# Layer 0 without key projection, one score fill for two key blocks, weights loaded in pieces, and another issue order

## What is computed

```python
# layer 0, per sequence: channels c = 64 tokens, positions s = 256 features, 8 heads
xn = layernorm_over_(c, s)(x) * gamma[:, None] + beta[:, None]
q  = Wq @ xn + bq                       # (8*64, 256)
k, v = split(Wkv @ ctx + bkv)           # (8*64, 256) each
att = softmax(q.T @ k / sqrt(64))       # per head, 256 x 256
x  = x + Wo @ (att @ v) + bo
# layer 1: queries from x, keys and values from layernorm(ctx), 16 heads of 16, gated
# layer 2: queries from ctx's partner x, keys and values from both (two key blocks), then an MLP
# layer 3: self-attention, cross-attention with ctx, MLP
```

## Time and profile before

| | |
|---|---|
| time, median of 3 runs | 1281.34 us (1281.11 to 1281.63) |
| span of the profiled execution, first to last instruction | 1279.4 us |
| TensorE (PE) busy | 1250.0 us, 98% |
| VectorE (DVE) busy | 1002.7 us, 78% |
| ScalarE (ACT) busy | 866.9 us, 68% |
| GpSimd (POOL) busy | 610.1 us, 48% |
| mean granted TensorE clock | 0.997 |

### The profile page before, as it was taken

The page is one execution under the profiler, slowest core; times in us unless marked ns, Lnnn a source line. Parts: engine busy times, 40 slices in busy tenths (PEclk is TensorE's granted clock), DMA queues, the critical chain, the costliest instruction groups (busy, mean ns, idle before and its releaser), DMA issues.

```text
span 1279.4 us, 35838 instructions
## 1 busy us (share of the span) xinstructions
PE 1250.0 (98%) x13338; PEld 988.7 (77%) x13338; DVE 1002.7 (78%) x2426; ACT 866.9 (68%) x2287; POOL 610.1 (48%) x1003
## 2 busy tenths in 40 slices
PE   8999999999999999999999999999999999998898
PEld 6777768777787787877878687877878787877777
DVE  4788797887888787897868878887887989676753
ACT  3777766676777677666786777677586677765452
POOL 2554454454545545554553744545454454443231
PEclk9999999999999999999999999999999999999999
DMA  9000000000000000000000000000000000000000
GB/s 340 23 19 19 1 20 7 23 8 6 19 11 20 7 22 7 7 19 11 19 6 12 20 6 20 7 11 21 10 15 11 19 7 6 3 6 2 5 6 5
DMA packets 23592, 25.82 MB, mean 20 GB/s; under 512 B 10624, under 2 KB 22912, under 8 KB 23168
## 3 DMA queue, kind: packets, MB, share of 16 engines
q1 hardware_dynamic: 22208, 22.89, 5.6%
q10 hardware_dynamic: 1216, 0.66, 0.3%
HBM read 21.44 MB, written 2.10 MB: 18 GB/s over the span
## 4 chain that ended last, share of the span: by engine, by line
PE 82%; DVE 6%; issue 4%; ACT 3%; POOL 3%; DMA 0%; POOLq 0%; ACTq 0%; DVEq 0%
PE bank L691 9%; PE bank L960 9%; PE bank L517 8%; PE attended L646 8%; PE bank L631 8%; PE bank L969 8%; PE bank L697 5%; PE bank L725 5%; PE bank L506 4%; PE bank L751 4%; PE bank L714 3%; PE bank L738 3%; PE bank L684 2%; PE bank L425 2%; PE bank L742 2%
## 5 line engine op out<-in xcount | busy, mean ns | idle before, releaser
L618 POOL TENSOR_SCALAR p_a<-p_a,rec_a 128x256 f32<-128x256 f32 x512 | 243.4, 493 | 184.3 <-DVE rec_a L573 182.8
L604 ACT ACTIVATE p_a<-bank,nmax_a 128x256 f32<-128x256 f32 x512 | 237.8, 480 | 63.3 <-DVE nmax_a L567 62.5
L567 DVE TENSOR_REDUCE nmax_a<-bank 128x2 f32<-128x512 f32 x256 | 167.0, 677 | 13.3 <-PE bank L517 12.9
L631 PE MATMUL bank<-ident,p_a 128*128 128x128 f32 x1024 | 146.1, 277 | 3.9 <-POOL p_a L618 3.5
L517 PE MATMUL bank<-k_a,q_a 64*128 64x256 f32 x1024 | 139.2, 397 | 1.5 <-ACT q_a L584 0.6
L631 PEld LDWEIGHTS bank<-ident,p_a 128*128 128x128 f32 x1024 | 115.4, 142 | 31.5 <-issue 20.9
L646 PE MATMUL attended<-p_a,v_a 128*64 128x256 f32 x1024 | 131.7, 389 | 1.8 <-DVE p_a L664 1.4
L517 PEld LDWEIGHTS bank<-k_a,q_a 64*128 64x128 f32 x1024 | 91.9, 186 | 31.0 <-issue 22.2
L679 ACT ACTIVATE p_a<-bank 128x512 f32<-128x512 f32 x128 | 77.2, 605 | 46.2 <-PE bank L631 45.2
L604 ACT ACTIVATION_READ_ACCUMULATOR p_a<-bank,nmax_a 128x1 f32 x512 | 107.9, 211 | 0.0
L646 PEld LDWEIGHTS attended<-p_a,v_a 128*64 128x64 f32 x1024 | 64.8, 136 | 49.6 <-issue 19.7
(11 more groups left out here) (263 smaller groups left out, 3034.0 us busy)
## 6 DMA issues: line engine op xcount, KB each, us to landing
wb<-in_wb SPq DMA_DIRECT2D x1, 4096.0 KB, 13.6
wc<-in_wc SPq DMA_DIRECT2D x1, 4096.0 KB, 24.0
xc<-in_x SPq DMA_DIRECT2D x16, 128.0 KB, 2.7
xc<-in_ctx SPq DMA_DIRECT2D x16, 128.0 KB, 2.9
c_top<-in_ctx SPq DMA_DIRECT2D x16, 128.0 KB, 2.8
k_c<-in_ctx SPq DMA_DIRECT2D x16, 128.0 KB, 2.0
res_a<-in_x SPq DMA_DIRECT2D x16, 128.0 KB, 2.1
out<-y_out SPq DMA_DIRECT2D x16, 128.0 KB, 1.7
```

The costliest lines, as they stand in the source:

```text
L567: dve.tensor_reduce(nmax_a[:, n, e, :], ps[:, :].rearrange("p (q k) -> p q k", q=KT), AX.X, ALU.max, negate=True).then_inc(A.s["max"], 1)
L604: last = act.activation(p_a[:, j % 2, n, e, qt, :], ps[:, qt * D:(qt + 1) * D], ACT.Exp, bias=nmax_a[:, n, e, qt:qt + 1], accum_out=sum_a[ ...
L618: last = pool.tensor_scalar(p_a[:, j % 2, n, e, qt, :], p_a[:, j % 2, n, e, qt, :], rec_a[:, n, e, qt:qt + 1], 1.0, ALU.mult, ALU.mult)
L631: last = nc.tensor.transpose(ps[:, kt * D + qt * P:kt * D + (qt + 1) * P], p_a[:, j % 2, n, e, qt, kt * P:(kt + 1) * P], ident[:, :])
```

## The change

1. **Layer 0's keys.** The setup makes `wm`, the product of each head's query and key weights (transposes of the loaded weights, line 1268, eight 64-wide matmuls, 1276), and `bq`, the key weights times the query bias (1279). x is loaded twice, into both 64-row halves of `xx`; ctx into both halves of `cc`. A new stage `q` makes the queries of a pair in two steps of two matmuls (510), ScalarE scales them (522), and line 539 scores them against the raw ctx in `cc`. The key projection and VectorE's `k_a` are gone. The queries of all four rounds have a place of their own in `q_a`; `xx` has one place instead of two.
2. **Stage `e`.** The scores of both key blocks go into the same four banks as one fill of 32 matmuls, after both blocks of keys are ready, and VectorE masks 512 columns with one instruction (the mask is spread over four heads, with zeros for the second block).
3. **Weights.** `wb` comes in eight pieces, `wc` in six; three pieces are issued by ScalarE, the others by SyncE, and each user waits for its own piece.
4. **Order.** All five order strings and the bank table are new. Filler matmuls: 13 + 62 instead of 14 + 97.

```diff
-WARM_UP = 14
-IDLE_WORK = 97
+WARM_UP = 13
+IDLE_WORK = 62
...
-    fills = [(("qk", j, 0), ("qk", j, 1)) for j in range(2)]
-    for u, j, n in units():
-        fills.append((("s", u, 0), ("s", u, 1)))
-        if n and j + 2 < H0 // 2:
-            fills.append((("qk", j + 2, 0), ("qk", j + 2, 1)))
-    return tuple(fills)
+    return tuple((("s", u, 0), ("s", u, 1)) for u, j, n in units())
...
+    "q": ((("q", 0), ("q", 1)), (("q", 2), ("q", 3))),
...
     "pe": (
-        "wwwwwwwwsnswwwwwwnnnaaaaaaddaaddddkdaasdksddnkddkdkksnaakkdddkaadddkdaddaadddnnabdadbdnadbdkddddnabadbdbdadkbd"
+        "wwwwwwwwwwwwwsnksssknnkqqanakkskdaanddkdddaadddsdnsddaddddaqddqaadkdddkkddnanaddbkbdndbdddaaddbdbddbaabkeddnee"
...
+        def pe_q(i):
+            pe, z = nc.tensor, i % 2
+            for p in range(2):
+                yield
+                if i == 0:
+                    written(X, pe, 0, ("m", 0))
+                    written(X, pe, 0, ("m", 1))
+                pe.wait_ge(N.s["norm"], N.at(i, "norm", 2))
+                for half, rows_ in enumerate((slice(0, S), slice(S, P))):
+                    ps = fill_bank(A, pe, i, ("q", 2 * p + half))
+                    filled(A, mm(ps[:, :], wm[rows_, p, :, :], xx[rows_, :, :], start=True, stop=True), i, ("q", 2 * p + half))
...
-                for half, rows_ in enumerate((slice(0, S), slice(S, P))):
-                    ps = fill_bank(A, pe, i, ("qk", j, half))
-                    filled(A, mm(ps[:, :], wqk[rows_, 2 * j:2 * j + 2, :], xc[rows_, z, :, :], start=True, stop=True), i, ("qk", j, half))
...
-                        ins = mm(bs[e][:, qt * D:(qt + 1) * D], q_a[rows_, j % 2, n, qt * P:(qt + 1) * P], k_a[rows_, j % 2, n, :],
+                        ins = mm(bs[e][:, qt * D:(qt + 1) * D], q_a[rows_, j, n, qt * P:(qt + 1) * P], cc[rows_, z, n, :],
...
-                ins = dve.tensor_scalar(k_a[:, j % 2, :, :], ps[:, :].rearrange("p (n s) -> p n s", n=2), bqk[:, 1, j:j + 1], None, ALU.add)
...
+            yield
+            written(T, pe, i, "q")
+            pe.wait_ge(T.s["kblk"], T.at(i, "kblk", 1))
+            if T is E:
+                pe.wait_ge(T.s["kblk_own"], T.at(i, "kblk_own", 1))
+            bs = [fill_bank(T, pe, i, ("s", g)) for g in range(QUADS)]
             for c in range(blocks):
-                yield
-                written(T, pe, i, "q")
-                kblk = "kblk_own" if T is E and c else "kblk"
-                pe.wait_ge(T.s[kblk], T.at(i, kblk, 1))
-                bs = [fill_bank(T, pe, i, ("s", c, g)) for g in range(QUADS)]
...
-            def masked(c, ps, dst):
-                if c == 0:
-                    return dve.scalar_tensor_tensor(dst, ps, 1.0 / HD, bc(m2[:, :], 1, HB // 2), ALU.mult, ALU.add)
-                return dve.tensor_scalar(dst, ps, 1.0 / HD, None, ALU.mult)
+            def masked(ps, dst):
+                return dve.scalar_tensor_tensor(dst, ps, 1.0 / HD, m2[:, :, :, :], ALU.mult, ALU.add)
...
-            sp.dma_start(wb[:, :], dram["wb"]).then_inc(setup["wb_in"], 16)
+            load_weights(sp, wb, "q0", "b_q0")
+            load_weights(sp, wb, "o0", "b_o0")
```

More of the change, by code:

```diff
@@ L44, with piece @@
 WCOLS = sum(a * b for a, b in WB.values())
+PIECES = {"q0": ("q0", "q0"), "kv0": ("k0", "v0"), "o0": ("o0", "o0"), "q1": ("q1", "q1"), "kv1": ("k1", "v1"), "o1": ("o1", "o1"),
+          "w1": ("w1", "w1"), "w2": ("w2", "w2"), "qkvo0": ("q0", "o0")}
+def piece(name):
+    sizes = {n: a * b for n, (a, b) in WB.items()}
+    names = list(sizes)
+    first, last = (names.index(n) for n in PIECES[name])
+    start = sum(sizes[n] for n in names[:first])
+    return slice(start, start + sum(sizes[n] for n in names[first:last + 1]))
 UNITS = H0
@@ L49 @@
 AHEAD = 4
-WARM_UP = 14
-IDLE_WORK = 97
+WARM_UP = 13
+IDLE_WORK = 62
 SHIFTED_APART = 13
 def attention_fills(blocks):
-    return (tuple(tuple(("s", c, g) for g in range(QUADS)) for c in range(blocks))
+    return ((tuple(("s", g) for g in range(QUADS)),)
             + tuple((("t", r, c),) for r in range(KT) for c in range(blocks)) + (("o",), ("p",)))
@@ L379, in place @@
         def place(T, i, name):
-            return places["d" if T is A and name[0] == "x" else T.name, i, name]
+            return places[{"x": "d", "q": "q"}.get(name[0], "a") if T is A else T.name, i, name]
         def fill_bank(T, eng, i, name):
@@ L1284, in pe_s @@
             pe = nc.tensor
+            halves = (slice(0, S), slice(S, P))
+            yield
+            pe.wait_ge(setup["consts"], IDENT)
+            pe.wait_ge(setup["wqk_in"], 32)
+            ps = fill_bank(X, pe, 0, "wT")
+            for j in range(H0 // 2):
+                last = pe.transpose(ps[:, j * P:(j + 1) * P], wqk[:, 2 * j:2 * j + 2, :].rearrange("p h o -> p (h o)"), ident[:, :])
+            filled(X, last, 0, "wT")
+            yield
+            pe.wait_ge(setup["cols_in"], 32)
+            written(X, pe, 0, "wT")
+            bs = [fill_bank(X, pe, 0, ("m", e)) for e in range(2)]
+            for j in range(H0 // 2):
+                for e, half in enumerate(halves):
+                    mm(bs[e][halves[j % 2], j // 2 * S:(j // 2 + 1) * S], wT[half, j, 0:S], wT[half, j, S:P], start=True, stop=True)
+            for j in range(H0 // 2):
+                for e, half in enumerate(halves):
+                    last = mm(bs[e][half, P + j:P + j + 1], wT[half, j, S:P], col("l0_bq")[half, 2 * j + e:2 * j + e + 1], start=True, stop=True)
+                    if j == H0 // 2 - 1:
+                        filled(X, last, 0, ("m", e))
             yield
@@ L1305, in pe_s, with load_weights @@
                 filled(X, last, 0, ("row", n + 1))
+        def load_weights(eng, tile, name, sem):
+            eng.dma_start(tile[:, piece(name)], dram["wb" if tile is wb else "wc"][:, piece(name)]).then_inc(setup[sem], 16)
         def act_s():
             yield
-            for dst, src in ((wv_raw[:, :, :], dram["wv0"]), (wo_raw[:, :, :], dram["wo0"])):
-                nc.scalar.dma_start(dst, src).then_inc(setup["wvo_in"], 16)
             for dst, src in ((wqk[0:S, :, :], dram["wq0"][0:S, :].rearrange("p (h c) -> p h c", c=P)[:, :, 0:S]),
```

403 lines of the change are left out of this document (201 added, 202 removed).

## The result

The change brings the time from 1281.49 us (median of 4 runs of the kernel before on the same chip, 1281.11 to 1282.12) to **1220.88 us** (4 runs, 1219.85 to 1221.77). The ratio is 0.9529, with a 95% interval of 0.9515 to 0.9542: 60 us faster, where 62 were forecast.

A forecast was written before the change was run, and what follows sets the result against it. TensorE, busy 1250.0 of 1279.4 us, was taken as the bound, so work removed from its middle is time. Terms -27.5 - 32 + 4 - 8.5 + 2 = -62 take 1281.3 to 1219 us, range 1207 to 1240.

The forecast's parts named there:

- the middle: From first projection to last layer-0 sum: -27.5 for the projection, -32 for switches, +2 for waits, -57.5 us in all.
- the tail: From the last layer-0 sum to the end: -8.5 us, from fewer fillers, idle time unchanged.
- The key projection: Layer 0 on TensorE: 64 of 128 wide matmuls go, 32 pairs at 0.86 us each, -27.5 us.
- Switches: TensorE's changes of tile shape fall from 660 to 454, at 0.155 us each: -32 us, the largest term.
- Rival A: Fewer tile-shape switches give little: only the drain counts, or savings return as PSUM bank waits; 1241 to 1249 us, chance 0.10.
- Setup: Start of the kernel: added weight products and transposes delay the first projection to about 21 us; net +4 us.
- Fillers: 36 fewer filler matmuls, all but one in the tail, 72 records of 0.118 us: -8.5 us.
- I let the idle time of the tail stand: End of the kernel: useful work behind the last layer-0 sum stays about the same, TensorE's idle time there too.
- Rival B: Gaps of the tail stay, 8.5 us return as idle, with clock dips: 1228, up to 1231 us; chance 0.11.
- The other engines: VectorE's dropped key copies, its wider masks, ScalarE's work and double x loads: worth nothing while TensorE bounds.
- New waits: Middle of the kernel: faster TensorE demand and stage e's joint fill add +2 us to 8.7 us of idle.
- below 12: Sign in the profile after: TensorE's idle time between 40 us and the tail stays below 12 us.

The follow-up runs named there:

- best matched pair of kernels: Changed kernel with 90 neighbouring TensorE steps exchanged, switches kept at 454 (1252.5 us), against the changed kernel with 90 exchanges adding 180 switches (1271.5 us).
- the narrow kernel: Kernel before, with layer 0's query and key projections of rounds 2 and 3 over 8 columns instead of 512: 1277.1 us.

## Why the prediction was right

The direction and the size are right, and the bulk of the mechanism with them: less busy time of TensorE, at nearly the same idle time. That the sum ends within 2 us of the measured time is luck, as the middle and the tail missed by 11 and 8 us in opposite ways. By its own steps:

1. **The key projection, -27.5.** The length of a visit came out as forecast, 0.86 and 0.96 us. Doubling it cost 23.0 of 27.5, so the term is worth 23 to 27.5.
2. **Switches, -32.** The largest term, and probably too large: 0.11 to 0.12 us each by the best matched pair of kernels and 0.11 to 0.13 by the middle, which is -22 to -27, though single comparisons give 0.09 and 0.16 and the fit over the rows 0.14 to 0.15. Rival A (1241 to 1249) is not what happened, but the error lies on its side. The Trainium skill (TensorE: Matmul & The Clock Gate, Part 2, What happens when you issue a matmul) has a drain of about 128 cycles, by an estimate 53 ns at 2.4 GHz. That is about half of what these kernels show for a switch, so the trace does not agree that it is all of the cost.
3. **Setup, +4.** The first projection started at 21.72, forecast 21. The parts were not: the 64x64 products ran in about 0.5 us, and work of other stages stands between. The clock had a part that the forecast left out. By their pace the rows of before run at the slower level up to 17.3 us (pairs of line 425 start 0.42 us apart, then 0.21), though the clock column reads 1.00 there; in the changed kernel the column has 0.50, the 1.2 GHz level, from 9.7 to 23.4 us, so its first projection ran slow as well, 1.92 us for two matmuls (the row at 21.72 above). That the total fits is luck in part. The setup, the weights in pieces and stage `e`'s joint fill were not tried alone.
4. **Fillers, -8.5.** The tail lost 16.8. In its ledger fillers are 8.3 of it (35 x 2 x 0.118), idle time 5, and most of the other 3.5 is work that now lies ahead of the last layer-0 sum. The fillers are not the cause: taking them all out of either kernel made it 4 to 6 us longer. What is left is the tail's new order, which puts work in the gaps, as the forecast said; no run tries that alone. "I let the idle time of the tail stand" was wrong, on the good side. The low end of the range had allowed for it. Rival B, idle growing to 24 us, is refuted: it fell to 10.9.
5. **The other engines, nothing.** Right for the key copies (1280.4 without half of them). Off for the masks: the wide one saves 3.5 us of VectorE's work (forecast: none) and 3.8 of the time.
6. **New waits, +2.** It was 4 between the two cuts. In the windows from 40 us on, which the forecast meant, it was 7 (8.7 to 15.7), over its "below 12". They are in no single place, and stage `e`'s fill has 3.0 us in all.

The range and the sign stood on the premise that a microsecond taken from TensorE is a microsecond. TensorE's ledger bears it out for the change as a whole: 60.1 us less busy, 59.4 less span. It does not hold for the work alone: 23 us taken from the old stream gave 4.8. The condition "as long as the others keep up" was written as one on their load (81% of VectorE). By these runs it is one on the order, as far as VectorE's copies can tell. The changed kernel has tables made for the shorter stream, and with 90 steps of them exchanged it loses half of the gain. So the 60 us belong to the shortened work together with the new tables, and these runs don't let them be divided between the two. The prediction was right because the change brought both; for the 23 us of the narrow kernel, put into the old tables, the same reasoning was wrong by 18.

## What to carry to other kernels

A TensorE that is 98% busy in a fixed order tells what added work costs (23.0 of 27.5 us here), not what removed work gives: that was 4.8 of 23 us under the old order. When steps are reordered, make a control that reorders as much and changes nothing else; here it cost 31.6 us and would otherwise have been put down to tile shapes. And before counting a removed matmul as a gain, see what runs in the other half of the array at the same time.

## What the runs showed of the hardware

- A matmul on one 64-row half was free beside one of the same length on the other half: with it cut from 512 to 8 columns, the 64-row work around it took 3.64 us where it had taken 3.65. Cutting 32 of them changed the time by at most 0.13% (ratio 0.9987 to 1.0006).
- A visit of two matmuls of 8 columns, one in each half, still takes 0.25 us (542.13 to 542.38), a quarter of the 512-column visit, so these narrow matmuls don't shrink in proportion. The end that meets another shape lies in both.
- A change of tile shape costs 0.09 to 0.16 us in this stream: 0.11 to 0.12 by the best matched pair of kernels, 0.14 to 0.15 by a fit over all groups.
- Without fillers the clock fell to 0.75 over the last 27 us of the changed kernel, and the two kernels became 6 and 4 us longer, though 15 us of filler work was gone in the one and 23 in the other (62 and 97 fillers, two records of 0.118 us each).
